# A layer norm's second half carried from the end of one stage into the next, and a scan's direct terms moved to the head of its matmul program

## What is computed

```python
x = _layernorm(x + _L0_ffn_ref(x, ...))      # squared-relu feed-forward, ternary weights
x = _layernorm(x + _L1_attn_ref(x, ...))     # selective scan (Mamba)
x = _layernorm(x + _L1_xattn_ref(x, ...))    # cross attention, 32 heads of 8
x = _layernorm(x + _L1_ffn_ref(x, ...))      # attention, one shared key/value head per token
x = _layernorm(x + _L2_attn_ref(x, ...))     # self attention, one head of 256
...
x = _layernorm(x + _L2_ffn_ref(x, ...))      # eight experts, ternary weights
x = _layernorm(x + _L3_attn_ref(x, ...))     # RWKV recurrence
x = _layernorm(x + _L3_xattn_ref(x, ...))    # mLSTM (gated memory)
x = _layernorm(x + _L3_ffn_ref(x, ...))      # gated feed-forward, 8-bit activations
```

## Time and profile before

| | |
|---|---|
| median of 3 runs | 1857.37 us (1854.47 to 1859.31) |
| profiled execution, its own time | 1856.92 us |
| its span, first to last instruction | 1855.1 us |
| mean granted TensorE clock | 0.871 |
| PE busy | 1560.2 us (84%) |
| DVE busy | 1302.5 us (70%) |
| ACT busy | 1044.3 us (56%) |
| POOL busy | 582.2 us (31%) |

### The profile page before, as it was taken

How to read it: one execution, slowest core, us unless ns; L and a number is a source line. 1 busy time by engine, 2 the same in 40 slices (tenths; PEclk the granted TensorE clock), 3 DMA queues, 4 the chain that set the end, 5 groups by cost and what they waited for, 6 DMA issues and landing times. The chain is left out here.

```text
span 1855.1 us, 26209 instructions
## 1 busy us (share of the span) xinstructions
PE 1560.2 (84%) x8965; PEld 932.3 (50%) x8965; DVE 1302.5 (70%) x2648; ACT 1044.3 (56%) x2072; POOL 582.2 (31%) x511
## 2 busy tenths in 40 slices
PE   7958899999999899799988878885899978547935
PEld 3643466666677553556563356662222245235613
DVE  4766877677666443788748649647999957765778
ACT  2123556556554324798837848535899933606835
POOL 0205443131310000898715230004893000334620
PEclk9979999999999899899989979897555579768968
DMA  5100000000000100111014331008999920011000
GB/s 224 28 3 29 1 1 1 1 1 0 1 1 0 49 17 24 35 57 47 23 30 103 70 94 24 27 1 228 159 187 183 185 48 1 7 44 48 2 0 24
DMA packets 213683, 93.03 MB, mean 50 GB/s; under 512 B 205968, under 2 KB 206992, under 8 KB 211888
## 3 DMA queue, kind: packets, MB, share of 16 engines
q1 hardware_dynamic: 213408, 90.97, 21.0%
q10 hardware_dynamic: 144, 0.40, 0.1%
HBM read 39.36 MB, written 1.11 MB: 22 GB/s over the span
## 5 line engine op out<-in xcount | busy, mean ns | idle before, releaser
L1091 POOL TENSOR_TENSOR ss_u<-dx,b_rows 128x512 f32<-128x512 f32 x128 | 159.2, 1280 | 237.6 <-POOLq L195 221.0
L786 ACT ACTIVATE gq_p<-gq_s,gq_bias,gq_rq 128x512 f32<-128x512 f32 x128 | 98.4, 773 | 119.3 <-DVE gq_bias L856 119.2
L1173 DVE TENSOR_TENSOR_SCAN ss_h<-ss_decay,ss_u 128x512 f32<-128x512 f32 x128 | 146.5, 1204 | 25.1 <-PE ss_ht L1131 18.0
L2149 ACT ACTIVATE qc_p<-qc_s,qc_bias,sq 128x1024 int16<-128x1024 f32 x128 | 154.0, 1204 | 16.5 <-DVE qc_bias L2115 6.4
L719 POOL TENSOR_TENSOR gq_xw<-gq_x,weights 128x512 f32<-128x512 f32 x48 | 67.9, 1414 | 294.9 <-ACT gq_x L746 294.2
L2113 DVE TENSOR_REDUCE qc_mx<-qc_s 128x1 f32<-128x1024 f32 x128 | 155.4, 1214 | 2.4 <-PE qc_s L2048 2.4
L2048 PE MATMUL qc_s<-kT,qT 64*128 64x512 bf16 x256 | 130.8, 618 | 12.8 <-ACT qc_p L2149 7.4
L1145 PE MATMUL ss_acc<-ss_hc,consts 128*128 128x512 f32 x256 | 131.5, 597 | 0.0
L654 PE MATMUL gq_s<-gq_KT,gq_QT 128*128 128x512 f32 x256 | 121.9, 599 | 3.6 <-ACT gq_p L786 3.6
L676 PE MATMUL gq_o<-gq_pT,gq_V 128*128 128x256 f32 x512 | 121.2, 379 | 1.4 <-DVE gq_pT L890 1.4
L853 DVE TENSOR_REDUCE gq_mx<-gq_s 128x1 f32<-128x512 f32 x128 | 88.2, 691 | 43.9 <-PE gq_s L654 43.4
(11 more groups left out here) (611 smaller groups left out, 3721.0 us busy)
## 6 DMA issues: line engine op xcount, KB each, us to landing
b_rows<-b_rows SPq DMA_DIRECT2D x16, 512.0 KB, 3.6
weights<-in_weights SPq DMA_DIRECT2D x1, 6152.0 KB, 17.2
weights<-in_weights SPq DMA_DIRECT2D x1, 5248.0 KB, 17.3
weights<-in_weights SPq DMA_DIRECT2D x1, 3072.0 KB, 10.0
weights<-in_weights SPq DMA_DIRECT2D x2, 1155.0 KB, 5.1
weights<-in_weights SPq DMA_DIRECT2D x1, 2156.0 KB, 7.5
qc_pT<-qc_p SPq DMA_TRANSPOSE x128, 3.3
weights<-in_weights SPq DMA_DIRECT2D x1, 1410.0 KB, 8.9
```

The source lines that it names most:

```text
L786: nc.scalar.activation(pr[c % 2][:, t, :], sc[t][:, :], ACT.Exp, bias=bias[:, c, t:t + 1], scale=rq[b % 2][:, t, u:u + 1], accum_out=sm[:, ...
L1091: nc.gpsimd.tensor_tensor(u_in[i % 3][:, :], dx[:, m, hf * HT:hf * HT + HT], rows.rows[c % 2][:, n % rows.NEACH, :], ALU.mult).then_inc(in ...
L1173: nc.vector.tensor_tensor_scan(h[group % 2][:, m, :], decay[i % 2][:].rearrange("p b t -> p (b t)"), u_in[i % 3][:, :], 0.0, ALU.mult, ALU ...
L2149: nc.scalar.activation(pi[i % R][:, :], sc[i % 3][:, :], ACT.Exp, bias=bias[:, i:i + 1], scale=sq[:, t, h:h + 1], accum_out=sm[:, i:i + 1] ...
```

## The change

In six places the second half's variance, root, normalise, turn and store are taken from the end of the stage (`Finish`) and issued by a new helper, `Carry`, within the next stage: `L0_ffn` to `scan_inputs`, `L1_xattn` to `L1_ffn`, `L1_ffn` to `L2_attn`, `L2_ffn` to `L3_attn`, `L3_attn` to `L3_xattn`, `L3_xattn` to `L3_ffn`. The means and variances move to a tile that outlives the stage (`g.mv`). The next stage's work on the second half waits for `carry.stored` or `carry.x`. From `L3_xattn` to `L3_ffn` the turn and the copies of both halves go altogether. Where transposes use 256-column PSUM tiles, the four turns and copies are of 256 columns each. In the scan, the direct terms of the first half (n = 0, `hf` = 0) move from `sums` to the head of TensorE's program.

```diff
@@ L0_ffn (L1_xattn, L1_ffn, L2_ffn, L3_attn alike)
-                fin.turn(1)
...
-                for half in range(2):
-                    fin.root(half)
-                    fin.store(half)
+                fin.root(0)
+                fin.store(0)
...
-                fin.variance(1)
-                fin.normalise(1)
@@ selective_scan, TensorE
+                def skip_of(hf, t):
+                    for m in range(CT):
+                        nc.tensor.matmul(acc[t][:, m * P:m * P + P], xc[:, m, hf * HT + t * P:hf * HT + t * P + P],
+                                         skip[:, m, :], start=(m == 0), stop=False)
+
                 def sums(k):
                     hf, n, t = order[k]
-                    if n == 0:
-                        pe.wait_ge(skips, CT)
-                        if hf == 1:
-                            pe.wait_ge(gated, t + 1)
-                        for m in range(CT):
...
+                    if hf == 1 and n == 0:
+                        pe.wait_ge(gated, t + 1)
+                        skip_of(hf, t)
...
+                pe.wait_ge(skips, CT)
+                for t in range(CT):
+                    skip_of(0, t)
                 for i in range(U + LAG + 2):
@@ L1_ffn, TensorE, ScalarE, VectorE
+                head_logits(0)
                 for t in range(3):
                     select(t)
+                for i in range(4):
+                    carry.turn(i)
+                pe.wait_ge(carry.stored, 4)
+                head_logits(1)
...
+                carry.root()
+                exponents(0)
+                for i in range(4):
+                    carry.store(i)
+                exponents(1)
...
-                choose_heads()
+                carry.variance()
+                choose_heads(0)
+                carry.normalise()
+                weigh_heads(0)
                 for t in range(NT):
+                    if t == 3:
+                        choose_heads(1)
+                        weigh_heads(1)
                     pick(t)
@@ L2_attn, TensorE, ScalarE, VectorE
+                    if i == 2:
+                        pe.wait_ge(carry.stored, 2)
                     if i < B:
                         project(i)
+                    if i == 0:
+                        carry.turn(0)
+                        carry.turn(1)
...
+                    if i == 0:
+                        carry.root()
                     if i < B:
                         take(i)
+                    if i == 0:
+                        carry.store(0)
+                        carry.store(1)
...
+                carry.variance()
+                add_bias(0)
+                carry.normalise()
                 for i in range(B + 2):
+                    if i == 1:
+                        dve.wait_ge(carry.x, 4)
+                        add_bias(1)
@@ L3_attn, TensorE, ScalarE, VectorE
                 for hf in range(2):
+                    if hf == 1:
+                        for i in range(4):
+                            carry.turn(i)
+                        pe.wait_ge(carry.stored, 4)
                     for m in range(2):
...
+                carry.root()
                 nc.scalar.activation(w[:, :], td, ACT.Exp).then_inc(wexp, 1)
                 act.wait_ge(signs, 3)
+                for i in range(4):
+                    carry.store(i)
                 for hf in range(2):
                     exponents(2 * hf)
...
+                carry.variance()
                 nc.vector.memset(o[:, :, :, 0:1], -1e38)
...
                 dve.wait_ge(signs, 3)
+                carry.normalise()
                 highest_of(0)
@@ L3_xattn, TensorE, ScalarE, VectorE
                 gate_products(0)
+                carry.turn(0)
+                carry.turn(1)
+                pe.wait_ge(carry.stored, 2)
                 gate_products(1)
...
-                fin.turn(0)
-                fin.turn(1)
...
+                carry.root()
                 store_gates(0)
+                carry.store(0)
+                carry.store(1)
                 store_gates(1)
...
                 fin.root(0)
                 square(3)
-                fin.store(0)
                 root(3)
-                fin.root(1)
-                fin.store(1)
...
+                carry.variance()
+                carry.normalise()
                 gate_steps(0)
@@ scan_inputs, TensorE, ScalarE, VectorE
+                z_product(0)
+                z_product(1)
+                carry.turn(0)
+                carry.turn(1)
+                z_product(2)
+                z_product(3)
+                pe.wait_ge(carry.stored, 2)
                 for m in range(CT):
                     x_product(1, m)
...
+                        gate(1)
+                        carry.store(0)
+                        carry.store(1)
+                        for t in range(2, CT):
                             gate(t)
...
+                carry.variance()
+                convolve(0, 0)
+                carry.normalise()
+                for i in range(1, 2 * CT):
+                    convolve(i // CT, i % CT)
@@ new helper
+class Carry:
+    def variance(self):
+        for t in range(4, NT):
+            last = nc.vector.bn_aggr(g.mv[:, t, :], g.stats[:, t, :])
+        self.link(last)
+        v = g.mv[:, 4:NT, 1]
+        nc.vector.tensor_scalar(v, v, LN_EPS, None, ALU.add).then_inc(self.var, 1)
...
+    def turn(self, i):
+        per = self.width // P
+        c, first = i % 2, i // 2 * per
+        nc.tensor.wait_ge(self.x, first + per)
+        if i >= 2:
+            nc.tensor.wait_ge(self.stored, i - 1)
+        for j in range(per):
+            last = nc.tensor.transpose(self.pt[i % 2][:, j * P:j * P + P], g.X[:, 4 + first + j, c * P:c * P + P], g.ident)
+        last.then_inc(self.turned, 1)
+
+    def store(self, i):
+        c, at = i % 2, 512 + i // 2 * self.width
+        nc.scalar.wait_ge(self.turned, i + 1)
+        nc.scalar.copy(g.XT[:, c, at:at + self.width], self.pt[i % 2]).then_inc(self.stored, 1)
```

## The result

| | before | changed | changed, measured again |
|---|---|---|---|
| median | 1855.95 us, then 1857.85 | 1826.32 us (1823.06 to 1828.33) | 1828.57 us (1826.91 to 1831.20) |
| ratio to before, 95% interval | | 0.9828 (0.9814 to 0.9843) | 0.9847 (0.9833 to 0.9861) |
| profiled execution, its span | 1855.1 us | 1821.2 us | 1825.1 us |
| mean granted clock | 0.871 | 0.885 | 0.881 |

What follows compares the result with a forecast made beforehand. The prediction saw engines idle for 4.92 us at a stage end, TensorE restarting at a low clock, and TensorE as the scan's bound. Seven terms summed to -22.9 us, 1834.0 from 1856.92, median 1834.5; range 1828 to 1843.

Steps and rivals of the forecast that it cites:

- feed-forward to scan inputs: End of the first feed-forward: products start 4.6 us earlier, normalisation costs 1.6, TensorE keeps the upper clock; -4.8 us.
- scan: Scan: 32 direct-term matmuls leave where TensorE is the bound and start in a hole at the head; -5.6 us.
- cross to shared-head attention: End of the cross attention: start 4.9 us earlier, ladder of transposes and copies +1.9, head products cheaper; -4.5 us.
- shared-head to self attention: End of the shared-head attention: start 4.5 us earlier, less eight transposes queued ahead of the first scores; -3.6 us.
- experts to recurrence: Start of the recurrence: carried copies wait for TensorE's 24 products and delay ScalarE's first exponents; a loss, +2.8 us.
- recurrence to gated memory: Start of the gated memory: 5.1 us earlier, but second gate products wait 4.0 for ScalarE's copies; -0.5 us.
- gated memory to last feed-forward: End of the gated memory: both halves' turn and copies go, and VectorE's wait for the root; -6.7 us.
- the recurrence gains as well: Rival, recurrence: a wait behind the late exponents takes them up, -4.2 us instead of +2.8; 1827.5 us, chance 0.08.
- the low clock that the rival needed: Rival "slower", scan: head burst, short pause, then a lasting low TensorE clock eats the gain; 1865 us, chance 0.03.
- only moved a wait: Rival, three stages with plain gains: something else sets the pace, so 12.9 us are lost; 1847 us, chance 0.10.
- the hand-over drops the clock: Rival, four stages: transposes with waits drop TensorE to 0.50 for 5 us, 2.5 us each; 1844 us, chance 0.08.

Runs made afterwards that it cites:

- e3_no_recur: Changed kernel with the carried end from the experts into the recurrence undone, all else as changed: 1827.71 us, ratio 0.9839 to the kernel before.
- e4_late_copies: Changed kernel with ScalarE's four carried copies in the recurrence moved behind the first unit's exponents and the copies of v: 1820.00 us, ratio 0.9800.
- e5: Changed kernel with ScalarE's two carried copies in the gated memory put ahead of the table load and softplus: 1824.44 us, ratio 0.9824.
- e8: Changed kernel with the recurrence's carried copies behind the first exponents and value copies, and the gated memory's ahead of the softplus: 1821.09 us, ratio 0.9807.
- e12: Changed kernel with 16 identity transposes in TensorE's rest at the two uncarried stage ends (self attention, quantised attention): 1822.74 us, ratio 0.9817.
- e6_keep_busy: Kernel before, no carries, with 16 identity transposes where TensorE rests for the second half's normalisation at stage ends: 1840.92 us, ratio 0.9912.
- e7_first: Kernel before with one carried end alone, from the first feed-forward into the scan's inputs: 1849.22 us, ratio 0.9953.

## Why the prediction was right or wrong

The terms, measured in the first profile from the last statistics (or last ScalarE copy) of one stage to that of the next; the last two meet at the gated memory's second gates (1675.53 and 1650.05):

| step | forecast | its ends | measured |
|---|---|---|---|
| feed-forward to scan inputs | -4.8 | -3.0 to -5.1 | -5.2 |
| scan | -5.6 | -4.1 to -5.9 | -5.6 |
| cross to shared-head attention | -4.5 | -2.5 to -4.8 | -3.2 |
| shared-head to self attention | -3.6 | -2.5 to -4.5 | -5.4 |
| experts to recurrence | +2.8 | +1.5 to +3.2 | +0.7 |
| recurrence to gated memory | -0.5 | -2.5 to +2 | -2.8 |
| gated memory to last feed-forward | -6.7 | -6 to -7 | -6.2 |
| sum | -22.9 | | -27.6 |
| in stages without an edit | 0 | | -6.3 |

In the second profile the seven steps measure -27.6 again, each to 0.1, and the stages without an edit -2.4.

*Right in mechanism and size*: the scan, the first end and the last. In the last, 4.62 came from the start, and 0.46 went to the normalisation beside the transposes. From the second gates to the last statistics the stage became 2.0 shorter. VectorE's wait of 2.81 for the root is gone there, as this row of the changed kernel without an idle time shows, so some 0.8 was lost elsewhere in that stretch; where, no run settles.

```profile
1759.04 0.34 DVE L3036 RECIPROCAL mc_var<-mc_var 128x32 f32<-128x32 f32 x1
```

*Experts to recurrence: the mechanism right, the size wrong.* The copies do stand ahead of the exponents, and the ladder took 2.1 (1566.52 to 1568.6) as worked out. But the 24 products took 10.37, not 12.06: this is the forecast's own other end, "+1.5 if they run at the upper level", and I took 2.8. VectorE's scan came 19.74 after the last statistics, 18.33 in the earlier trace rows: +1.41. Another 0.7 was made good behind it; where, no run settles. e3_no_recur says the whole is worth 0.2 to 0.5. The rival "the recurrence gains as well" was wrong for this kernel: it is what the mended order gives (e4_late_copies).

*Recurrence to gated memory: the level again.* The first gate products took 5.26 (to the turns at 1640.94), the case of -2.5, and 3.72 passed from there to the second set, 4.0 by the forecast. The prediction had put the middle of the range on a lower level and on a clock lost in the pause; the level stayed at 1.00. ScalarE's bias ends at 1641.72 and the softplus starts at 1643.04, 1.32 later, so here too there is room for the load of 1.28 and none for the 1.38 us drain that the Trainium skill's page "ScalarE: Activation LUTs", What ACT_TABLE_LOAD costs, adds.

*Shared-head to self attention.* The start came 4.29 earlier. I had charged 0.9 for eight transposes ahead of the first scores; with 0.79 instead of 0.60 the scores came 12.76 after the first product, 13.17 before (the earlier trace rows and the row below), and the stage's own eight turns took 1.25, 1.97 before. Timeline of the kernel before, then of the changed one:

```profile
1206.58 1.89 PE L1833 MATMUL si_s<-si_kT,si_qT 128*128 128x256 f32 x8
...
1250.59 1.97 PE L3731 MATMUL si_s<-consts,X 128*128 128x128 f32 x8 [2.72 <-DVE X L3720]
```

```profile
1226.04 1.25 PE L3788 MATMUL si_s<-consts,X 128*128 128x128 f32 x8 [2.72 <-DVE X L3777]
```

*Cross to shared-head attention: too large here, too small in other profiles.* The ladder took 2.08 (1.9 forecast) and the second sixteen head products 1.81 (1.7). What I missed is that the twelve key and value products between them stayed low longer, 8.19 (1053.62 to 1061.81) instead of 7.36. Timeline of the kernel before:

```profile
1078.60 7.53 PE L1508 MATMUL sh_s<-weights,XT 128*128 128x512 f32 x12
1085.96 1.03 PE L1516 MATMUL sh_t<-weights,XT 128*128 128x256 f32 x4
```

In e5, e8 and e12, with the same program in this stage, those products took 6.6, the level did not fall behind the ladder, and the stage took 115.8: by those profiles the term is -6.4. So -4.5 lies between two values that the level decides, and that it is not further off is luck. An earlier start does not always bring the level with it.

*The failed step* is the size of three terms: at the ends into the self attention, the recurrence and the gated memory I took TensorE's level after the hand-over from its level after the long rest, or from the middle between the two, though the same prediction had noted that the rest shrinks from 3.5 to 1.3 us. These starts ran at 0.79, 1.00 and 1.00 instead of 0.60, 0.72 and 0.74, and the three terms came out 1.8, 2.1 and 2.3 us better than forecast; the four others together 1.5 worse. Where I followed that note (scan inputs) the term held. e6_keep_busy shows the level as a cause of its own: keeping TensorE at work through the rests is worth 16 us with no carried work. It can't be added to the carries; part of it is what the carries gained.

*A second step, put at nothing without a reason*, is the stages without an edit. With the measured 27.6 in place of 22.9 the forecast would have been 1829.8, inside the range. What took the first median below it lies there: in the first profile 6.3 us, 3.0 ahead of the first edit, 3.0 in the scan's output stage and the cross attention, 2.2 in the last feed-forward, less 1.9 in the quantised attention and the experts. In the second profile it was 2.4, the last feed-forward going the other way. I treat these as the level's chance from one execution and one kernel to the next; that is argued, not shown. For the cross attention's first 7.5 us, at 1.00 in all twelve profiles in which the first carried or busy end comes before it, the cause stays open. Medians, not one profile, are therefore the time to forecast.

*A sum of the prediction* is off with nothing hanging on it: 22 scans in 28 us make 5.1 us for a group of four, not 5.2, and the low clock that the rival needed did not come.

*The other rivals*: nothing only moved a wait, since the three plain gains were 5.2, 3.2 and 5.4; in the shared-head attention the level fell for some 4 us behind the ladder, as "the hand-over drops the clock" has it, but in one stage and not in four, and there in four of the seven profiles with this order; the scan's low clock did not come (0.90 from 738.87 to 754.87, against 0.63 from 746.94 to 762.94 before).

## What to carry to other kernels

Price a removed rest twice: the time by which the next stage starts earlier, and the level at which TensorE then works, read from the granted clock of the stage's first microseconds. Where an end can't be carried, idle transposes through its rest are worth a trial (e6_keep_busy, e12_after_busy). And when work is handed over, put its copies where that engine's queue has nothing urgent behind them: the same carry into the recurrence lost 0.2 to 0.5 us in one order and gained 6.2 in another (e3_no_recur, e4_late_copies).

## What the runs showed of the hardware that I had not expected

- Sixteen 128x128 transposes of a constant, 1.91 us of work in a rest of 3.5, hold the granted clock at 1.00 into the next stage (e6_keep_busy: scan inputs, self attention, gated memory; e12_after_busy: quantised attention, experts), but not always: after rests of 1.98 and 0.98 the recurrence still fell to 0.72.
- The clock of a stage can differ between kernels that are the same there: the cross attention's first 7.5 us were at 1.00 in e7_first, whose one edit lies 270 us ahead, and at 0.67 before, 2.6 us apart. That the edit is the cause is not shown.
- Two executions of one program differ by 3.6 us in one stage (55.56 and 59.12), at 0.68 and 0.50 over the same 10 us of it, and a stretch that no edit reaches took from 137.8 to 143.1 us over these kernels. A difference of that size between two single profiles says nothing about an edit.
